# A two-layer Mamba block on one core: a second operand buffer for the exponents, and weight loading through four staging areas

## The reference

```
h = layernorm(x) * (1 + ca) + sa
for two layers:                       # Mamba-2, 16 heads of 64, state 64
    u   = layernorm(h, w, b)
    z, xBC, dt = split(u @ in_w.T)    # 1024 | 1024 + 64 + 64 | 16
    dt  = softplus(dt + dt_bias)
    x, B, C = split(silu(conv4(xBC) + conv_b))       # causal, 4 taps
    state_t = exp(dt_t * A) * state_(t-1) + (dt_t * x_t) B_t ;  y_t = state_t C_t + D * x_t
    y   = y * silu(z);  y = y * rsqrt(mean(y*y) + eps) * rms_w
    h   = h + y @ out_w.T
x = x + ga * h
h = layernorm(x) * (1 + cb) + sb
x = x + gb * sigmoid(xr @ W_r.T) * (square(relu(xk @ W_k.T)) @ W_v.T)    # xr, xk mix a token with the one before
```

## Time and profile before

| | |
|---|---|
| median of 3 runs | 4825.02 us (4823.98 to 4826.77) |
| profiled execution | 4828.47 us, span 4826.7 us |
| PE busy | 4096.1 us (85% of the span), mean granted clock 0.953 |
| DVE, ACT, POOL busy | 3357.0, 2922.8, 2002.1 us |
| prologue | to about 133 us |
| layer 0: opening, 31 windows to the last one's exponents, last window | 133.2 to 236.8, to 2085.8, to 2134.5 |
| layer 1: the same | 2136.9 to 2240.8, to 4096.3, to 4147 |
| channel mix | to 4826.7 |

### The profile page before, as it was taken

The page is one execution under the profiler, slowest core; times in us unless marked ns, Lnnn a source line. Parts: engine busy times, 40 slices in busy tenths (PEclk is TensorE's granted clock), DMA queues, the critical chain, the costliest instruction groups (busy, mean ns, idle before and its releaser), DMA issues. The chain is left out here.

```text
span 4826.7 us, 100096 instructions
## 1 busy us (share of the span) xinstructions
PE 4096.1 (85%) x38872; PEld 3622.3 (75%) x38872; DVE 3357.0 (70%) x5217; ACT 2922.8 (61%) x4904; POOL 2002.1 (41%) x1572
## 2 busy tenths in 40 slices
PE   4399888888889899956989898989898998499999
PEld 1388888888878788846878888888888888377777
DVE  7377777777777777745777777777777777466664
ACT  4466666666666666635666666666666666466664
POOL 7134333333333334421333343434343444466664
PEclk6699999999999999978999999999999999699999
DMA  8300000000000000020000000000000000322220
GB/s 310 105 27 28 28 28 28 28 28 28 28 28 28 28 28 28 23 73 26 28 28 27 28 27 28 27 28 27 28 27 28 27 29 28 110 83 88 83 87 36
DMA packets 108673, 220.99 MB, mean 46 GB/s; under 512 B 10760, under 2 KB 11272, under 8 KB 107272
## 3 DMA queue, kind: packets, MB, share of 16 engines
q1 hardware_dynamic: 108176, 214.25, 12.6%
HBM read 146.97 MB, written 67.24 MB: 44 GB/s over the span
## 5 line engine op out<-in xcount | busy, mean ns | idle before, releaser
L501 PE MATMUL l_ring<-l_u_hi,l_wi_lo 128*128 128x256 f32 x4608 | 1312.9, 285 | 81.0 <-ACT l_raw L742 72.4
L501 PE MATMUL l_ring<-l_u_lo,l_wi_hi 128*128 128x256 f32 x4608 | 1298.1, 282 | 0.0
L501 PE MATMUL l_ring<-l_u_hi,l_wi_hi 128*128 128x256 f32 x4608 | 1296.9, 281 | 0.0
L974 DVE SCALAR_TENSOR_TENSOR l_xc<-l_raw,l_prm,l_xc 128x256 f32<-128x256 f32 x1536 | 852.3, 596 | 232.6 <-ACT l_xc L751 214.4
L501 PEld LDWEIGHTS l_ring<-l_u_hi,l_wi_lo 128*128 128x128 f32 x4608 | 876.4, 190 | 105.7 <-ACT l_raw L742 85.9
L501 PEld LDWEIGHTS l_ring<-l_u_lo,l_wi_hi 128*128 128x128 f32 x4608 | 876.1, 190 | 8.9
L501 PEld LDWEIGHTS l_ring<-l_u_hi,l_wi_hi 128*128 128x128 f32 x4608 | 874.6, 190 | 0.0
L1149 POOL TENSOR_TENSOR l_g<-l_g 128x512 f32<-128x512 f32 (+2 forms) x384 | 347.0, 904 | 926.8 <-ACT l_g L812 906.7
L1120 POOL TENSOR_TENSOR l_rhs<-l_cum,l_small 32x1024 fp32r<-32x1024 f32 x256 | 496.3, 1939 | 514.8 <-PE l_wide L563 474.1
L1006 DVE TENSOR_TENSOR l_e<-l_e,l_ps_m 128x1024 f32<-128x1024 f32 x256 | 312.8, 1222 | 414.2 <-ACT l_e L800 410.2
L501 PE MATMUL l_ring<-l_wo_hi,l_g_lo 128*128 128x512 f32 x1024 | 411.9, 402 | 82.9 <-DVE l_g_lo L1026 82.9
(11 more groups left out here) (162 smaller groups left out, 8335.2 us busy)
## 6 DMA issues: line engine op xcount, KB each, us to landing
l_hn<-h_scratch SPq DMA_DIRECT2D x64, 512.0 KB, 4.0
l_res<-h_scratch SPq DMA_DIRECT2D x128, 256.0 KB, 3.8
h_scratch<-l_res SPq DMA_DIRECT2D x128, 256.0 KB, 2.1
m_rows<-in_x SPq DMA_DIRECT2D x16, 1024.0 KB, 9.5
h_scratch<-m_rows SPq DMA_DIRECT2D x16, 1024.0 KB, 7.7
f_x<-in_x SPq DMA_DIRECT2D x16, 1024.0 KB, 6.1
f_h<-h_scratch SPq DMA_DIRECT2D x16, 1024.0 KB, 8.2
out<-f_x SPq DMA_DIRECT2D x64, 256.0 KB, 2.0
```

What stands on the lines that cost most here:

```text
L501: last = nc.tensor.matmul(out, a, c, start=(k == 0), stop=(k == n - 1))
L974: ins = nc.vector.scalar_tensor_tensor(out=acc, in0=raw[:, k, tap:tap + TB], scalar=prm_sb[:, w:w + 1], in1=acc, op0=ALU.mult, op1=ALU.add)
```

## The change

`rhs` gets two buffers, one for the even and one for the odd chunks; POOL's `moving` waits for the exponents of two chunks before, and runs one chunk further ahead. On PE the odd exponents move up behind the first projection that follows the even ones, and projection 5 moves behind outputs(1,0). On ACT `decays` of the odd chunks moves ahead of `z_read` and `new_state`. In the opening the 12 pieces go through four areas (the halves of `zs`, and the tiles `xc` and `g`); the matrix constants are loaded after the fourth piece; the normalisation of the first rows comes ahead of the remainders; PE transposes the rows at once and projects when the eight `in_w` pieces are split; the four `out_w` pieces are split after u, ahead of `step_exp`.

```diff
-        rhs = sb("rhs", [P, NH, CH], F32R)
+        rhs = sb("rhs", [P, 2, NH, CH], F32R)
-        s_stage = [sem("stage0"), sem("stage1")]
+        s_stage = [sem(f"stage{k}") for k in range(4)]
         stage = [zs[:, k].rearrange("p k t -> p (k t)") for k in range(2)]
+        stage += [xc[:].rearrange("p k t -> p (k t)"), g[:].rearrange("p j k t -> p (j k t)")]
+        n_in, n_all = 2 * KD, len(pieces)
...
 sync:
-            sp.dma_start(e[:].rearrange("p a h t -> p (a h t)")[:, 0:K_ID], cst[:, 0:K_ID]).then_inc(s_cst, 16)
             for n, (kind, k, c0, w) in enumerate(pieces):
-                if n >= 2:
-                    sp.wait_ge(s_wlo, len(pieces) * layer + n - 1)
+                if n == 4:
+                    sp.dma_start(e[:].rearrange("p a h t -> p (a h t)")[:, 0:K_ID], cst[:, 0:K_ID]).then_inc(s_shape, 16)
+                if n >= 4:
+                    sp.wait_ge(s_wlo, n_all * layer + n - 3)
-                sp.dma_start(stage[n % 2][:, 0:w], source).then_inc(s_stage[n % 2], 16)
+                sp.dma_start(stage[n % 4][:, 0:w], source).then_inc(s_stage[n % 4], 16)
...
 tensor:
-            pe.wait_ge(s_cst, 32 * (layer + 1))
-            pe.wait_ge(s_wlo, len(pieces) * (layer + 1))
-            pe.wait_ge(s_init, layer + 1)
-            pe.wait_ge(s_cst_copy, 3 * (layer + 1))
+            pe.wait_ge(s_cst, 16 * (layer + 1))
             input_T(b0, 0)
+            pe.wait_ge(s_wlo, n_all * layer + n_in)
...
                 exponents(b, s, 0, 0)
                 proj(0)
+                exponents(b, s, 0, 1)
                 proj(1)
                 states(b, s, 0, 0)
                 outputs(b, s, 0, 0)
-                exponents(b, s, 0, 1)
                 proj(2)
                 states(b, s, 0, 1)
                 outputs(b, s, 0, 1)
                 front(b, s, 1, n1)
                 exponents(b, s, 1, 0)
                 proj(3)
+                exponents(b, s, 1, 1)
                 proj(4)
-                proj(5)
                 states(b, s, 1, 0)
                 outputs(b, s, 1, 0)
-                exponents(b, s, 1, 1)
+                proj(5)
...
+            pe.wait_ge(s_wlo, n_all * (layer + 1))
+            pe.wait_ge(s_init, layer + 1)
+            pe.wait_ge(s_cst_copy, 3 * (layer + 1))
             loop(pe, body)
 scalar:
                     step_exp(*nxt)
                     conv_in(*nxt, 0)
+                decays(b, s, 0, 1)
+                if n1:
                     z_read(*nxt, 0)
                 new_state(b, s, 0, 0)
-                decays(b, s, 0, 1)
...
                 high_g(b, s, 0)
+                decays(b, s, 1, 1)
                 if n1:
                     z_read(*nxt, 2)
+                new_state(b, s, 1, 0)
                 square_g(b, s, 0)
                 if n1:
                     conv_in(*nxt, 2)
-                new_state(b, s, 1, 0)
-                decays(b, s, 1, 1)
-                if n1:
                     silu_bc(*nxt)
...
             u_read(b0, 0, (0, 1))
+            for n in range(n_in, n_all):
+                split_high(n)
+            act.wait_ge(s_wlo, n_all * (layer + 1))
             step_exp(b0, 0)
 vector:
             norm_all(b0, 0)
+            for n in range(n_in):
+                split_low(n)
+            dve.wait_ge(s_shape, 16 * (layer + 1))
+            nc.vector.tensor_copy(rhs[:].rearrange("p a h t -> p a (h t)"),
+                                  stage_c[:, K_RHS:K_LHS].unsqueeze(1).broadcast_to([P, 2, NH * CH])
+                                  ).then_inc(s_cst_copy, 1)
+            nc.vector.tensor_copy(lhs[:].rearrange("p c t -> p (c t)"), stage_c[:, K_LHS:K_ID]).then_inc(s_cst_copy, 1)
             split_u(b0, 0)
+            for n in range(n_in, n_all):
+                split_low(n)
             steps(b0, 0)
 gpsimd:
-                pool.wait_ge(s_arg, n)
+                pool.wait_ge(s_arg, at_least_0(n - 1))
-                nc.gpsimd.tensor_tensor(rhs[0:32], cum[0:32, s % 2, c * CH:(c + 1) * CH].unsqueeze(1)
+                nc.gpsimd.tensor_tensor(rhs[0:32, c % 2], cum[0:32, s % 2, c * CH:(c + 1) * CH].unsqueeze(1)
...
-                moving(b, s, 1)
+                moving(b, s, 2)
                 skip_term(b, s, 0)
-                moving(b, s, 2)
+                moving(b, s, 3)
                 if n2:
                     inv_std(*nxt2)
                 skip_term(b, s, 1)
                 gate(b, s, 0)
-                moving(b, s, 3)
+                if n1:
+                    moving(*nxt, 0)
                 squares(b, s, 0)
                 if n1:
-                    moving(*nxt, 0)
+                    moving(*nxt, 1)
                 inv_rms(b, s, 0)
```

More of the change, by code:

```diff
@@ L386, in mamba_layer @@
         ident, one = const(K_ID, P), const(K_ONE, 1)
-        s_cst, s_prm = sem("cst"), sem("prm")
-        s_stage = [sem("stage0"), sem("stage1")]
+        s_cst, s_prm, s_shape = sem("cst"), sem("prm"), sem("shape_cst")
+        s_stage = [sem(f"stage{k}") for k in range(4)]
         s_whi, s_wlo, s_wsc = sem("w_hi"), sem("w_lo"), sem("w_scaled")
@@ L563, in exponents @@
                     last = nc.tensor.matmul(wide[:, 0 if odd else 1, n * 512:(n + 1) * 512], lhs[:, c, :],
-                                            rhs[:].rearrange("p h t -> p (h t)")[:, n * 512:(n + 1) * 512],
+                                            rhs[:, odd].rearrange("p h t -> p (h t)")[:, n * 512:(n + 1) * 512],
                                             start=True, stop=True)
@@ L678, in _, with split_high @@
             act.wait_ge(s_prm, 16 * (layer + 1))
-            act.wait_ge(s_cst, 32 * (layer + 1))
+            act.wait_ge(s_cst, 16 * (layer + 1))
             nc.scalar.activation(a_neg[:], prm_sb[:, C_ALOG:C_ALOG + 1], ACT.Exp).then_inc(s_aexp, 1)
-            for n, (kind, k, c0, w) in enumerate(pieces):
-                act.wait_ge(s_stage[n % 2], 16 * (len(pieces) // 2 * layer + n // 2 + 1))
-                st = stage[n % 2][:, 0:w]
+            def split_high(n):
+                kind, k, c0, w = pieces[n]
+                act.wait_ge(s_stage[n % 4], 16 * (n_all // 4 * layer + n // 4 + 1))
+                st = stage[n % 4][:, 0:w]
                 if kind == "out":
@@ L877, in _ @@
         def _(dve):
[L878 to L881, removed]
+            dve.wait_ge(s_cst, 16 * (layer + 1))
             eye = bti[:].rearrange("n c (a t) -> n (c a) t", a=2)
@@ L891, in _, with split_low @@
             nc.vector.tensor_scalar_mul(a_neg[:], a_neg[:], -1.0).then_inc(s_aneg, 1)
-            for n, (kind, k, c0, w) in enumerate(pieces):
-                dve.wait_ge(s_whi, len(pieces) * layer + n + 1)
-                nc.vector.tensor_tensor(piece_at(n, wi_lo, wo_lo), stage[n % 2][:, 0:w],
+            def split_low(n):
+                kind, k, c0, w = pieces[n]
+                dve.wait_ge(s_whi, n_all * layer + n + 1)
+                nc.vector.tensor_tensor(piece_at(n, wi_lo, wo_lo), stage[n % 4][:, 0:w],
                                         piece_at(n, wi_hi, wo_hi).bitcast(F32), ALU.subtract).then_inc(s_wlo, 1)
@@ L1090, in _ @@
             norm_all(b0, 0)
+            for n in range(n_in):
+                split_low(n)
+            stage_c = e[:].rearrange("p a h t -> p (a h t)")
+            dve.wait_ge(s_shape, 16 * (layer + 1))
[3 more added lines that the diff above has]
+            nc.vector.tensor_copy(lhs[:].rearrange("p c t -> p (c t)"), stage_c[:, K_LHS:K_ID]).then_inc(s_cst_copy, 1)
             split_u(b0, 0)
+            for n in range(n_in, n_all):
+                split_low(n)
             steps(b0, 0)
@@ L1173, in body @@
                 inv_rms(b, s, 1)
-            pool.wait_ge(s_cst, 32 * (layer + 1))
+            pool.wait_ge(s_cst, 16 * (layer + 1))
             pool.wait_ge(s_prm, 16 * (layer + 1))
@@ L1179, in _ @@
                 if s:
+                    pool.wait_ge(s_wlo, n_all * (layer + 1))
+                if s:
                     moving(b0, 0, 0)
+                    moving(b0, 0, 1)
                 inv_std(b0, s)
```

## The result

The changed kernel took 4685.6 us (median of 4 runs, 4679.6 to 4687.7), the kernel before 4825.9 (4 runs, 4824.0 to 4827.3): ratio 0.9708, 95% interval 0.9691 to 0.9724. The forecast was 4683. The profiled execution took 4687.65 us with a span of 4685.8, 140.8 less than the profiled one of before.

| | before | after | gain |
|---|---|---|---|
| SP's first issue of the layer to the first window's T | 103.6 / 103.9 | 78.2 / 77.2 | 52.0 |
| the 31 periods T to T | 1849.0 / 1855.5 | 1806.0 / 1812.0 | 86.5 |
| last window, T to its last result | 48.64 / 48.61 | 47.02 / 47.01 | 3.2 |
| everything else | | | -0.9 |

What follows compares the result with a forecast made beforehand. Bounds: in windows, the chain from first exponents to square sum; in openings, a chain of short hand-overs. 88.7 + 1.2 + 4.5 + 48 = 142.4 off 4825.0 gave 4683 us, 8-in-10 range 4660 to 4710.

Steps and rivals of the forecast that it cites:

- The window: In each window with projections, the way from first exponents matmul to square sum shrinks 37.79 to 36.36, gaining 1.43 us.
- e(0,1): ACT's exp of the odd chunk in a window ends 10.36 us after the first exponents matmul, 1.55 earlier.
- the wait before exponents (1,1): New PE wait of 1.1 us behind projection 3, for DVE's x_read(1).
- The term 88.7 + 1.2: Gain of the 62 windows with projections: 1.43 us each, plus 0.6 more in each layer's last but one.
- the tails: The 20.82 us from a window's square sum to the next window's first exponents, left in order except one POOL instruction.
- Rival 4: x_read(1) is no bar, PE runs through and a window gains 2.5 us: 4616; chance 0.04.
- POOL: The four moving instructions per window, in new places, cost 0; range nothing to 1.9 us for one on the chain.
- Rival 3: PE's clock falls at the mid-projection wait in every window, costing 2.6 us each: 4844; chance 0.03.
- The port: In the opening, POOL's extra moving beside DVE's row statistics costs nothing; if it stopped DVE, 1.9 us per layer.
- The opening: Each layer's opening gains 24 us, 48 in all, bounds 13 and 27; step_exp at 170.3 is 26.2 early.
- the charge of 2.2 for the clock: Deduction per opening for PE's lowered clock after idling 4 to 5 us behind projections 0 and 1.
- Last windows: Each layer's last window, without projections, gains 2.25 us from earlier e(0,1) and moved exponents (1,1), 4.5 in all.

Runs made afterwards that it cites:

- Experiment 3: The changed kernel with ACT's exp of the odd chunk again behind the z read and state copy: 4782.4 us.
- experiment 4: The changed kernel with exponents (1,1) one projection later on PE, behind projection 4 instead of 3: 4600.8 us.
- experiment 6: The changed kernel with DVE's row statistics behind x_read of head 1 and POOL's inverse deviation behind gate 0: 4607.5 us.
- Experiment 5: The changed kernel, two rhs buffers kept, with POOL's body in the order of before: 4950.7 us.
- Experiment 8: The changed kernel with four staging areas but the opening's old order (all pieces, then norm; PE waits for all pieces): 4706.2 us.
- experiment 9: The kernel of experiment 6 with DVE's taps of the third conv part ahead of the mean square: 4518.0 us.
- experiment 10: The kernel of experiment 9 with ACT's high half and square of the second gated product each moved earlier: 4491.4 us.
- experiment 11: The kernel of experiment 10 with a second buffer for v, so the second u_read needn't wait for the first split_u: 4352.3 us.

## Why the prediction was right

*The window.* Point by point: exponents (0,1) at T+3.66 forecast, T+3.73 measured; e(0,1) T+10.36 and T+10.36; `x_read` T+20.17 and T+20.17; the wait before exponents (1,1) 1.1 and 0.99; e(1,1) T+23.4 and T+23.28; square sum T+36.36 and, as the median of the 62 windows, T+36.42. The term 88.7 + 1.2 for the 62 windows measured 86.5, 3.4 less. Added up over the windows, the way from T to the square sum gained 88.2, and the tails behind it, which the forecast left as they were, took 1.8 more. 1.0 of that is idle time at the loop's turn (40.7 before, 41.7 after, in 11 turns). Experiment 3 shows that all of the gain hangs on e(0,1), experiments 4 and 6 that the new wait has the place and about the price given to it, and that the chain through `x_read` is what bounds.

*Rival 4* (2.5 per window if `x_read` were no bar, 4616) did not happen, but experiments 4 and 6 made its condition true and measured 4601 and 4607. By the periods they gained 2.73 and 2.64 per window over the kernel before, so its price was nearly right.

*POOL* was taken as nothing, and with its new order no matmul of the changed kernel waits for `rhs`. But the forecast treated the order as a detail. Experiment 5 shows that it carries the change: with POOL's old order the second buffer makes the kernel 2.6% slower than before. The text priced what moving (3) would do to DVE, and never what PE pays if it is late.

*The clock.* Rival 3 gave 2.6 per window if the clock fell at the new wait, a price taken from the idle of 4.02 in the earlier trace rows. It did not fall: the idles of about 1 leave the clock of the window at 1.00, as the earlier trace rows said. Behind experiment 5's idle of 3.63 it fell, and that stretch took 1.55 longer per window.

*The port.* Beside the opening's second moving (POOL, 179.63 to 181.53) DVE's statistics ran at 0.69 each, 1.29 the pair, as in a window, so the forecast of nothing held. In the window the two L969 took 2.08 beside a moving that ended at 1057.60, and the second of them ended 0.08 behind it; it is off the chain, DVE idles 3.99 soon after. In experiment 6, where POOL was idle at that place, both took 0.35. That is the rule of the Trainium skill (SBUF — State Buffer, SBUF: two separate sides) that the loser of the shared port blocks to the end of the other's instruction; the trace agrees with it for the statistics (not slowed), for L969, and for the tap of 1.98 beside the gate, where a tap alone takes 0.48.

*The opening.* Forecast 24 per layer, measured 25.4 and 26.6. The points: first high part at 139.4 and 139.66; norm done at 143 and 142.2; last low part 155 and 155.9; first projection 160 and 160.64; step_exp 170.3 and 170.33. The last agreement is partly luck. The second four pieces came 2.7, 2.1 and 1.4 apart, not 1.4 each. The last low part was 0.9 late, and that was made up by shorter copies (1.22 + 0.42 instead of 1.8) and by `out_w` pieces that took less than 2.45 each (9.36 for the four on ACT).

The term mis-sized is the charge of 2.2 for the clock. From SP's first issue step_exp came 26.3 and 27.0 earlier, and T 25.4 and 26.6 earlier: the charge cost 1.0 and 0.3. PE did stand idle, 5.19 and 5.79, and the clock did fall: from step_exp to T it was 0.82 and 0.80, before 0.88 in both layers. Experiment 8, without that idle, kept 0.88 and 0.87 and needed 40.4 from step_exp to T, the changed kernel 41.36 and 40.67. In layer 0 ACT got the first conv input of 128x512 2.4 later behind step_exp than before, so the charge was there at first. Then it fell into waits that had been longer:

```profile
214.28 0.58 PE L501 MATMUL l_ring<-l_u_hi,l_wi_lo 128*128 128x256 f32 x1 [2.57 <-ACT l_raw L742]
```

```profile
189.18 0.39 PE L504 MATMUL l_ring<-l_u_hi,l_wi_lo 128*128 128x256 f32 x1 [1.17 <-ACT l_raw L750]
```

The first row is of before, the second of after. ACT's wait for the taps just ahead of this shrank as much, from 4.18 to 2.78. That the opening's rest is paced by the taps was the forecast's reason for charging less than 2.6; it should have charged less still.

*Last windows.* 2.25 each forecast, 1.6 measured. The way to the square sum gained 2.7, more than forecast. The step that failed is that the rest would stay as it was. The second out product took 1.0 longer, at a lower granted clock, in layer 0 before and after (columns of the earlier trace rows):

```profile
2125.36:2132.80 7.44, 7.42 (x26) 5.92 (x26) 0.00 (x0) 0.95 (x1) 2.47 (x3) 0.78 0.00 0
```

```profile
2054.49:2062.90 8.41, 8.41 (x26) 6.68 (x26) 0.00 (x0) 0.94 (x1) 2.46 (x3) 0.66 0.01 2
```

The mean clock of the whole last window was 0.75 before and after and hides this.

*The sum.* That 4683 came within 3 us of 4685.6 is partly luck: by the profiled executions the openings gained 4.0 more than forecast, the 62 windows 3.4 less, the last windows 1.3 less and everything else 0.9 less.

## What to carry to other kernels

A buffer and an order are one change: count for each engine when it will now produce what the second buffer holds. When a chain's head is moved, follow it to the next wait, and move that wait's cause too; here the wait left behind was worth nearly what the windows' part of the change had brought (78 us against 87), and experiments 9 to 11 took 255 more behind it. Some 37 of the 255 came at the loop's turn, beyond what the other windows gained. Price a wait of TensorE with its clock: here 1.0 us cost itself, 3.63 cost 5.2, but in experiment 9 the clock fell behind 1.22.

## What the runs showed of the hardware

- TensorE's clock fell in experiment 5 behind an idle of 3.63 us, to 0.63 over the next 4.3 us. In experiment 9 it fell (0.62 over 4.5 us) where the longest idle was 1.22, while experiment 6, with idles of 1.15, 1.15 and 0.61 in the same tail, kept 1.00. What tells these apart stays open.
- At a granted 0.5 a projection's 256 columns started every 0.21 us, at 1.00 every 0.117.
- The idle at the loop's turn, 4.02 in the earlier trace rows and 3.7 to 4.2 in experiment 6, was still 3.5 to 4.0 in experiment 9. With the edits of experiment 10 it was 1.3 to 1.8, in experiment 11 1.3 to 1.9, where the turn's windows took 53.6 to 55.1 against 52.7. Nothing in those edits is aimed at it, and its cause wasn't tried.
- The last window of a layer, with the same code, took 43.6 at a clock of 0.88, 44.9 at 0.85 and 47.0 at 0.75. It differs from one kernel to the next and between the layers of one run, by up to 3.5 us (47.1 and 43.6 in experiment 4). That bounds how well sums of a few us per layer can be tested.
